# First tile's activations ahead of the second expert tile's weight conversion, and four token stores moved ahead of SyncE's wait for the last inverses

## The reference, cut to what matters

```python
h = _layernorm(x, axis=-1) * (1 + ca) + sa
x = x + ga * _L0_attn_ref(h, L0_attn_qkv_w, L0_attn_qkv_b, L0_attn_proj_w, L0_attn_proj_b)
h = _layernorm(x, axis=-1) * (1 + cb) + sb
x = x + gb * _L0_ffn_ref(h, L0_ffn_gate_w, L0_ffn_gate_b, L0_ffn_expert_bias, L0_ffn_w1, L0_ffn_b1, L0_ffn_w2, L0_ffn_b2)

# _L0_ffn_ref: top_idx = argmax of the gate logits; for each expert e
mask = (top_idx == e)[..., None].astype(x.dtype)
h = jax.nn.relu(jnp.einsum('bsd,df->bsf', x, w1[e]) + b1[e])     # 256 -> 1024
y = jnp.einsum('bsf,fd->bsd', h, w2[e]) + b2[e]                  # 1024 -> 256
out = out + mask * y
```

## Time and profile before

| | us |
|---|---|
| median of 3 runs | 1901.31 |
| lowest, highest of the 3 | 1901.19, 1902.53 |
| the profiled execution's own time | 1898.18 |
| its span from first to last instruction | 1896.4 |
| PE busy | 1792.0 (94%) |
| DVE busy | 1658.1 (87%) |
| ACT busy | 1413.7 (75%) |
| POOL busy | 564.5 (30%) |
| mean granted TensorE clock, of full speed | 0.956 |

### The profile page before, as it was taken

The page is one execution under the profiler, slowest core; times in us unless marked ns, Lnnn a source line. Parts: engine busy times, 40 slices in busy tenths (PEclk is TensorE's granted clock), DMA queues, the critical chain, the costliest instruction groups (busy, mean ns, idle before and its releaser), DMA issues. The chain is left out here.

```text
span 1896.4 us, 38503 instructions
## 1 busy us (share of the span) xinstructions
PE 1792.0 (94%) x15332; PEld 896.2 (47%) x15332; DVE 1658.1 (87%) x1803; ACT 1413.7 (75%) x2642; POOL 564.5 (30%) x406
## 2 busy tenths in 40 slices
PE   7976999999999999999999999999999994899997
PEld 4542333333333333333333333333333364899997
DVE  6769799999999999999999999999998475688886
ACT  1330788888888888888888888888888641678785
POOL 1105411151224115123411521331182015344442
PEclk8985799999999999999999999999999985899999
DMA  6666011241151233115113311511113734788873
GB/s 194 232 159 134 14 58 62 65 83 48 48 110 54 69 65 76 48 49 115 60 57 67 73 47 67 98 64 54 48 50 128 215 118 143 240 272 281 273 245 116
DMA packets 142660, 208.57 MB, mean 110 GB/s; under 512 B 42442, under 2 KB 87789, under 8 KB 140688
## 3 DMA queue, kind: packets, MB, share of 16 engines
q1 hardware_dynamic: 130608, 178.92, 32.8%
q0 software_dynamic: 7520, 18.80, 3.5%
q10 hardware_dynamic: 4352, 8.39, 1.2%
HBM read 122.10 MB, written 73.06 MB: 103 GB/s over the span
## 5 line engine op out<-in xcount | busy, mean ns | idle before, releaser
L1245 DVE TENSOR_REDUCE att_mx<-att_PM 128x2 f32<-128x1024 f32 x1024 | 1245.2, 1225 | 70.7 <-PE att_PM L1102 63.7
L1213 ACT ACTIVATE att_probs<-att_PS 128x512 f32<-128x512 f32 x2048 | 1111.7, 596 | 191.6 <-PE att_PS L1089 152.8
L1135 PE MATMUL att_PV<-att_probs,att_VU 128*32 128x256 f32 x8192 | 655.7, 392 | 7.7 <-ACT keep_sums L1234 6.2
L1089 PE MATMUL att_PS<-att_QE,K 50*128 50x512 f32 x2048 | 535.4, 498 | 2.0 <-ACT att_probs L1213 1.8
L1102 PE MATMUL att_PM<-K,QM 50*128 50x512 f32 x2048 | 438.9, 413 | 21.9 <-DVE att_mx L1245 15.0
L1089 PEld LDWEIGHTS att_PS<-att_QE,K 50*128 50x128 f32 x2048 | 203.1, 184 | 433.6 <-ACT att_probs L1213 410.6
L1135 PEld LDWEIGHTS att_PV<-att_probs,att_VU 128*32 128x32 f32 x8192 | 162.7, 108 | 369.0 <-issue 201.8
L979 POOL CAST att_mh<-att_m 128x16 fp32r<-128x16 f32 x32 | 6.3, 197 | 807.3 <-DVE att_m L1252 807.3
L1102 PEld LDWEIGHTS att_PM<-K,QM 50*128 50x128 f32 x2048 | 206.0, 191 | 44.4 <-DVE att_mx L1245 36.5
L576 POOL TENSOR_TENSOR QM<-QS,QM 16x1024 fp32r<-16x1024 f32 x62 | 146.6, 2364 | 8.5 <-POOL QM L995 6.1
L567 POOL TENSOR_TENSOR K<-KS,K 16x4096 fp32r<-16x4096 f32 x14 | 125.2, 8940 | 1.8 <-POOL K L1006 1.3
(11 more groups left out here) (217 smaller groups left out, 1602.3 us busy)
## 6 DMA issues: line engine op xcount, KB each, us to landing
H<-in_w SPq DMA_DIRECT2D x44, 1024.0 KB
routed_rows<-att_filling SPq DMA_DIRECT2D x32, 1088.0 KB, 4.3
att_QE<-QM SPq DMA_DIRECT2D x32, 512.0 KB, 3.0
QS<-qkT SPq DMA_DIRECT2D x186, 64.0 KB, 2.4
KS<-qkT SPq DMA_DIRECT2D x42, 256.0 KB, 9.2
qkT<-KS ACTq DMA_DIRECT2D x16, 512.0 KB, 5.6
all_X<-routed_rows SPq DMA_DIRECT2D x20, 258.0 KB
all_X<-in_x SPq DMA_DIRECT2D x4, 1024.0 KB, 9.9
```

The lines of the kernel that those rows point to most:

```text
L1089: nc.tensor.matmul(PS[score_bank(i)][:], K[r % BODY // CHUNKS][rows, ab, kt * P:(kt + 1) * P], QE[r % 2][rows, ab, :], start=True, stop=Tr ...
L1135: last = nc.tensor.matmul(PV[32 * h:32 * h + VW, cols], VU[r // CHUNKS % 2][:, j, h, :], probs[:, j % SLOTS, h, cols], start=j == 0 and ha ...
L1213: nc.scalar.activation(probs[:, kt % SLOTS, h, :], PS[score_bank(i)][:], ACT.Exp).then_inc(exps, 1)
L1245: nc.vector.reduce_max(mx[:, r % 2, at:at + 2, kc], PM[bank][:], AX).then_inc(maxima, 1)
```

## The change

Two independent parts. In `tail`, SP stores lots 0 to 3 directly behind the load of the first expert's first weights, ahead of its wait for the last inverses; lots 4 to 7 stay where they were. In `experts`, ACT converts the second tile's first weights after the first tile's ReLUs and the copy of the second tile's transposed rows, and DVE takes their low part ahead of that of the second tile's second weights.

```diff
@@ tail, block.sync
+            def keep_lot(i):
+                sp.wait_ge(added, 2 * i + 2)
+                sp.dma_start(g.x2[i * CH:(i + 1) * CH, 0:D].rearrange("(t p) d -> p t d", p=P), g.X[:, lot(i), :]
+                             ).then_inc(g.x2_in, 16)
+
...
             sp.dma_start(g.w1_first, g.first_weights[0].rearrange("p (k f) -> p k f", k=KD)).then_inc(g.in_w1, 16)
+            for i in range(CHUNKS):
+                keep_lot(i)
             sp.wait_ge(g.inverted, UNITS - 1 + CHUNKS)
             store_last_inverses(sp, g, CHUNKS - 1)
             load_second_heads(sp, g, CHUNKS - 1)
...
-            for i in range(LOTS):
-                sp.wait_ge(added, 2 * i + 2)
-                sp.dma_start(g.x2[i * CH:(i + 1) * CH, 0:D].rearrange("(t p) d -> p t d", p=P), g.X[:, lot(i), :]
-                             ).then_inc(g.x2_in, 16)
+            for i in range(CHUNKS, LOTS):
+                keep_lot(i)
@@ experts, block.scalar
             copy_turned(0)
-            first_weights(1)
             for k in range(NT):
...
                 if there(k + 1):
                     copy_turned(k + 1)
+                    if k == 0:
+                        first_weights(1)
                     second_weights(k + 1)
@@ experts, block.vector
                 if there(k + 1):
                     low_rows(k + 1)
+                    if k == 0:
+                        for c in range(PIECES):
+                            first_low(1, c)
                     low_weights(k + 1)
-                if k == 0:
-                    for c in range(PIECES):
-                        first_low(1, c)
```

## The result

The changed kernel takes **1894.04 us** (median of 11 executions, 1889.08 to 1898.84), the kernel before 1900.09 in the same group of runs (11, 1896.56 to 1902.53). The ratio is 0.9972, 95% interval 0.9960 to 0.9984: faster, by 0.28% or some 5 us. The prediction said 14 us. 1894.04 lies within its range and near rival 1 (1894.7): the experts' part works and the tail's part gives nothing. Two executions far from all others, 8435.65 us in e1 and 2119.42 of the kernel before beside it, are left out of the ratios. The profiled execution takes 1894.33 us (span 1892.6).

What follows compares the result with a forecast made beforehand. PE was taken to bound the kernel, with dips at the first expert tile and tail. Profiled 1898.2 - 6.6 (experts) - 7.7 (tail) = 1883.9, plus 0.3 for clock, plus 3.1 to the median: 1887.3 us; range 1883.5 to 1896.

Steps and rivals of the forecast that it cites:

- rival 1: Tail gives nothing, only experts gain, because the counts stay late: 1894.7 us, chance 0.32.
- I take that coincidence for a cause: Tail: PE's counts come late when eight stores beside POOL's scatters fill the DMA engines; admitted as unproven by the trace.
- part 2: Tail: early stores of lots 0 to 3 make counts prompt and POOL go straight on, 7.7 us gained.
- late counts: Tail: work that PE's rows show as done is counted some 4 us later and more, holding up ACT and DVE.
- the gap: Tail: POOL's 8.00 us idle between scatter rounds 1 and 2, waiting for DVE; its removal was put at 7.7 us.
- Part 1: Experts: ACT's wait and conversion leave the path ahead of the first tile's ReLUs; 6.6 us gained, between 4.9 and 7.9.
- the 1.3 given back: Experts, tile 2's layer 2: waits of about 1.0 at the second pair and 0.3 at the fourth reduce 7.9 to 6.6.
- the bound of 3: Experts, tile 2: upper bound in us on the time given back, if weights land 2 us later by sharing the engines.
- The inverses' stores: SP's queue: these small stores start behind 2.1 MB of early stores, 0.2 to 2.9 us late, mostly swallowed by a reserve.
- The 3.1 us: Whole kernel: amount by which the median of the runs was taken to lie above the profiled time.
- late only in the execution that is recorded: Tail: a possible reason why the tail gives nothing; the timed runs never had the loss.

Runs made afterwards that it cites:

- e1: The kernel before with the experts' part of the change alone: 1896.83 us, ratio 0.9974 to the kernel before.
- e3: The changed kernel with the stores of lots 4 to 7 behind all scatters and the first rows' load: 1902.39 us, ratio 1.0006 to the kernel before.
- e13: The kernel before, unchanged, a fourth time for its profile: one execution, 1896.01 us.
- e2: The changed kernel with the experts' part undone, leaving only the tail's early stores: 1899.11 us, ratio 0.9994 to the kernel before.
- e9: The changed kernel with POOL waiting behind its first eight scatters for the gates of lots 4 and 5, run again: 1902.37 us, ratio 1.0006 to the kernel before.
- e8: The kernel before, unchanged, run again for its profile; it took 1899.44 us in this group of runs.
- e7: The changed kernel, unaltered, run a second time: 1894.20 us, ratio 0.9975 to the kernel before.
- e11: The kernel before, unchanged, a third time for its profile; it took 1894.24 us in this group of runs.
- e10: The changed kernel, unaltered, run a third time: 1887.77 us, ratio 0.9974 to the kernel before.
- e4: The changed kernel with POOL's first scatter held back until round 2 is settled: one execution, 1914.34 us.
- e5: The changed kernel with POOL waiting behind its first eight scatters for the gates of lots 4 and 5: 1889.25 us, ratio 0.9992 to the kernel before.
- e14: The changed kernel with plain stores of the rows in token order in place of the 32 scatters, run again: one execution, 1883.20 us.

## Why the prediction was wrong

- **The step that failed** is "I take that coincidence for a cause": full DMA engines, filled by the eight stores, make the counts late. Emptying them left the wait at 9.63 us (e3, share 0.27), and the unchanged kernel has full engines without the wait (e13, share 1.04). With it fell the 7.7 us of part 2; e2 measures 0.9994, a gain of at most 0.26% or 5 us by its interval.
- **The price of the late counts** was right: I put 7.7 on the gap, the profiles differ by 8.2 and the levels by 7.7. What I couldn't see in one profile is that they belong to the group of runs and not to the program.
- **My argument against rival 1**, that scatters from 1587 on go with prompt counts, was true of that profile but is no property of scatters: in e9 the late counts came in just that place.
- **Part 1** was right in mechanism: ReLUs 3.0 us behind the matmuls, no idle, full clock, layer 1 of tile 2 13.9 us behind tile 1's. Its size, 6.6, measured 6.0 at tile 3 in the first profile, but 3.9 and 4.6 between e8 and e7 and between e11 and e10 (33.94 and 30.08; 34.16 and 29.57). The mis-sized term is the 1.3 given back. At tile 2 the gains are 8.5, 7.8 and 8.4 (7.9 predicted), so what is given back by tile 3 measures 2.5, 3.9 and 3.8, in two of three above the bound of 3. ACT of e10, the third tile's first weights:
```profile
1627.32 2.00 ACT L1842 CAST keep_w_hi<-H 128x1024 fp32r<-128x1024 f32 x2 [4.20 <-DMA H<-in_w]
```
They are converted 17.4 us behind tile 1's layer 1 (16.3 in the first profile), and layer 2 of tile 2 then waits 2.9 in all (1.78, 0.70, 0.17, 0.21), 3.0 in e7. I had named weights that share the engines with the next ones as what could make this term 3, and took too little of it. That the sharing makes them late is argued, not tested. To the last layer 2 the gains are 5.5, 4.2 and 5.6 (268.33 and 262.79; e8 268.33, e7 264.13; e11 268.99, e10 263.41; 6.1 with e13, 269.53, in place of e11) and 4.5 between e2 and e1 (268.55 and 264.03), and the three ratios, 0.9972, 0.9975 and 0.9974, give 5.0.
- **The inverses' stores** behind 2.1 MB in the queue: priced at 0.2 to 2.9 late, measured nothing beyond the 1.5 us by which that whole stretch is later: the loads behind those stores follow 3.34 us behind them, 3.32 before. The burst falls from 346 GB/s to 59 at about 1549.5, just as they are issued, so next to nothing was left ahead of them. The rule of the Trainium skill that I set against this half (DMA: Bandwidth & Descriptors, Queues, rings and completion order) was therefore not put to the test.
- **The median** came out at 1894.04 because the experts' part gives 5 to 6 and the tail's 0: rival 1, which had 0.32. That it lies within 0.7 us of that rival's time is partly luck: the rival starts from 1901.3 and takes off 6.6, where the kernel before took 1900.09 and the medians differ by 6.05. The 3.1 us that I put between the profiled execution and the median isn't a fixed distance either: in the changed kernel the median is 0.3 below. Of rival 1's two reasons, "the scatters make the counts late" stays open, and "late only in the execution that is recorded" isn't borne out as far as runs that all record can tell: levels and profiles go together.

**What stays open** is what makes a group of runs late. Seen: where it is late, the first late count is of lot 4's gates, which end 10 to 11 us behind the start of a run of scatters, and DVE is released 2.3 to 3.5 us behind its end (changed kernel: 1583.27 against 1579.92 and 0.96). In e2 and e8 the last of lot 5's gates itself ends only then and is counted at once, so there only ACT's counts were late. Without scatters beside the gates the lateness was absent (e4). It was absent too beside the scatters of e4's lot 7 and in the second run of scatters of the first profiles; in two groups of five it never came. The chip recorded for the prompt group of e5 has the same number, 13, as that of the late e1 to e4 (15 for e7 to e9, 10 for e10 to e14), so it isn't tied to the number alone.

## What to carry to other kernels

Convert or load for the next tile behind the activations of this one when the matmuls wait for them; what bounded the gain here was how late the weights of the tile after next were converted. Before a wait in one profile is priced as the program's, see whether it stands in a second profile from another group of runs. And an experiment is read against a neighbour profiled beside it: e5 alone would have "shown" a cure that e9 disproved. And a wait of the predicted size is no proof of the term: here the shown waits summed to 1.4, the time given back to 2.5.

## What the runs showed of the hardware

- In three groups of runs counts of TensorE's finished work reached ACT and DVE late, with waits of 2.1 to 12.6 us `<-remote`: 3.0 us behind the end of lot 4's gates in the first profile (1571.58 against 1568.59), 14 behind that of lot 7's in e9. In two groups, with the same programs, no such wait stands there. The median time of the kernel before differs by 7.7 us of 1900 (0.4%) between the two kinds, more than the change gives.
- GpSimd issues a scatter of 128 rows each 1.3 us (31 steps in 40.28 us, e11). Where the counts are prompt it never rests from the first to the last (e11), so there, once the first round is settled, the scatters set the tail's length, and faster gates or choices of the later rounds would not shorten it.
- With DMA engines at 0.88 to 1.04 of their time (e11 and e13, 1557.4 to 1576) TensorE's counts were prompt.
